# Graph attention feeding a graph convolution: a bias added by an accumulating DMA, and some second-layer tiles computed in rounded halves

## What is computed

```python
# layer 0, per batch                      # layer 1
h  = input @ W                            support = x @ W1 + b
e  = f1 + f2.T          # h@a1, h@a2      y = adj @ support
e  = where(e >= 0, e, 0.2 * e)            mean, var over all batches and nodes
attention = softmax(adj * e, axis=1)      y = relu((y - mean) * rsqrt(var + eps) * gamma + beta)
x  = attention @ h + bias + input         out = y + x
```

## Time and profile before

| | us |
|---|---|
| three runs, median (lowest to highest) | 909.66 (909.13 to 911.93) |
| the profiled execution | 911.96 |
| its span, first to last instruction | 910.2 |
| busy in the span: PE | 871.0 |
| ACT | 804.2 |
| DVE | 726.1 |
| POOL | 211.6 |

### The profile page before, as it was taken

How to read it: one execution, slowest core, us unless ns; L and a number is a source line. 1 busy time by engine, 2 the same in 40 slices (tenths; PEclk the granted TensorE clock), 3 DMA queues, 4 the chain that set the end, 5 groups by cost and what they waited for, 6 DMA issues and landing times.

```text
span 910.2 us, 8919 instructions
## 1 busy us (share of the span) xinstructions
PE 871.0 (96%) x3167; PEld 547.5 (60%) x3167; DVE 726.1 (80%) x794; ACT 804.2 (88%) x614; POOL 211.6 (23%) x166
## 2 busy tenths in 40 slices
PE   6999999999999999999999999999999999999960
PEld 4335556675656756676566756567566765666850
DVE  3655788797878888887877978788888978879966
ACT  5998699988999799998999889997999979997645
POOL 0012214250333112341142401341113411323000
PEclk9999999999999999999999999999999999999995
DMA  8996676748677595867767495775957677565988
GB/s 337 422 362 240 260 291 237 292 165 334 224 273 268 203 360 173 294 234 267 280 237 300 155 357 207 267 274 199 358 174 292 231 263 287 192 224 190 423 335 344
DMA packets 46220, 246.39 MB, mean 271 GB/s; under 512 B 5560, under 2 KB 6184, under 8 KB 19552
## 3 DMA queue, kind: packets, MB, share of 16 engines
q1 hardware_dynamic: 46176, 245.82, 71.7%
HBM read 221.57 MB, written 24.23 MB: 270 GB/s over the span
## 4 chain that ended last, share of the span: by engine, by line
PE 83%; DVE 7%; ACT 3%; issue 2%; DMA 2%; SPq 1%; POOL 0%; DVEq 0%; ACTq 0%; POOLq 0%
PE acc L526 40%; PE acc L499 10%; PE acc L493 10%; PE acc L495 10%; DVE exp_lo L765 4%; PE acc L480 4%; PE acc L507 2%; PE acc L454 2%; PE acc L539 1%; PE acc L542 1%; PE acc L541 1%; ACT scores L623 1%; DMA adj_slot<-biasT 1%; DVE stats L786 1%; ACT hi L637 1%
## 5 line engine op out<-in xcount | busy, mean ns | idle before, releaser
L746 DVE CUSTOM_DVE_ANT_0 scores<-scores,adj_slot 128x2048 f32<-128x2048 f32 x128 | 297.5, 2324 | 77.5 <-ACT scores L616 30.2
L765 DVE SCALAR_TENSOR_TENSOR exp_lo<-scores,rz,hi 128x2048 fp32r<-128x2048 f32 (+1 forms) x133 | 280.5, 2125 | 0.0
L616 ACT ACTIVATE scores<-adj_slot,f_cols 128x2048 f32<-128x2048 f32 x128 | 255.0, 1998 | 15.4 <-PE acc L499 11.8
L623 ACT ACTIVATE scores<-scores,neg_mx 128x2048 f32<-128x2048 f32 x128 | 255.1, 1993 | 14.2 <-DVE neg_mx L749 14.2
L637 ACT ACTIVATE hi<-scores,rz 128x2048 fp32r<-128x2048 f32 (+1 forms) x133 | 227.5, 1726 | 33.6 <-DVE rz L758 30.4
L526 PE MATMUL acc<-adj_slot,region_even 128*128 128x512 f32 x512 | 228.8, 592 | 0.0
L526 PE MATMUL acc<-adj_slot,region_odd 128*128 128x512 f32 x392 | 175.3, 592 | 0.8 <-DVE region_odd L801 0.8
L526 PEld LDWEIGHTS acc<-adj_slot,region_even 128*128 128x128 f32 x512 | 96.7, 190 | 99.7 <-issue 95.7
L499 PE MATMUL acc<-exp_lo,h_hi 128*128 128x512 f32 x448 | 121.5, 391 | 0.8 <-DVE exp_lo L765 0.7
L526 PEld LDWEIGHTS acc<-adj_slot,region_odd 128*128 128x128 f32 x392 | 74.0, 190 | 77.2 <-issue 73.2
L495 PE MATMUL acc<-hi,h_hi 128*128 128x512 f32 x448 | 119.9, 390 | 0.0
(11 more groups left out here) (77 smaller groups left out, 614.7 us busy)
## 6 DMA issues: line engine op xcount, KB each, us to landing
adj_slot<-adjT SPq DMA_DIRECT2D x159, 1024.0 KB, 5.1
adj_slot<-xT SPq DMA_DIRECT2D x20, 1024.0 KB, 7.6
adj_slot<-biasT SPq DMA_DIRECT2D x32, 256.0 KB, 6.5
xp_dram<-adj_slot SPq DMA_DIRECT2D x32, 256.0 KB, 2.6
adj_slot<-xp_dram SPq DMA_DIRECT2D x8, 1024.0 KB, 12.1
adj_slot<-f_rows SPq DMA_DIRECT2D x7, 1024.0 KB, 6.9
adj_slot<-y_dram SPq DMA_DIRECT2D x7, 1024.0 KB, 12.0
outT<-adj_slot SPq DMA_DIRECT2D x6, 1024.0 KB, 4.7
```

The source lines that it names most:

```text
L616: act.activation(scores[t % ER][:, :], slots[f1_slot(bt.par)][:, :], ACT.Prelu, bias=f2_cols[:, bt.n, t:t + 1], alpha=ALPHA).then_inc(edge ...
L623: act.activation(scores[e][:, :], scores[e][:, :], ACT.Exp, bias=neg_mx[:, e:e + 1], accum_out=zsum[:, e:e + 1]).then_inc(exp_done, 1)
L746: dve.tensor_tensor_reduce(scores[e][:, :], scores[e][:, :], slots[s][:, :], 1.0, NEG_BIG, ALU.mult, ALU.max, mx[:, e:e + 1]).then_inc(max ...
L765: dve.scalar_tensor_tensor(exp_lo[e][:, part_cols(t, i)], scores[e][:, part_cols(t, i)], rz[:, e:e + 1], hi[m][:, part_cols(t, i)].bitcast ...
```

## The change

**The bias.** Its four loads and POOL's four adds go. Once the residual has landed, POOL issues one DMA that adds the bias from DRAM to it in SBUF. `make_xp` waits for that DMA for all four chunks.

**Lent slots.** Slot 9, no longer the bias's, and slots 2, 3 and 4 are given to tiles by parity (`SWAP`): tiles 2, 3 and 4 of a batch take the slots that tiles 9, 11 and 10 of the batch before do not need any more in layer 0, and so are loaded before the batch begins (`load_early`). Tiles 8, 9, 10 and 11 of the previous batch are loaded again at k = 3, 4, 5 and 6.

**Halves.** In a steady batch the second-layer tiles k = 3, 7, 9, 11 and 14 (only 11 and 14 where batch 0 is the previous one: 32 tiles in all) are computed in three float32r passes (`layer1_halves`). The rounded half of the tile comes by a DMA of POOL's queue that rounds on the way (`load_hi`), a second 1 MB read of the tile, into a slot lent for it. DVE makes the low half in place (`tile_low`, one 128 x 2048 instruction each), at its steps 1, 4, 6, 8 and 11, and POOL makes the halves of the tile's 128 columns of support (`split_support`, two instructions each). The slots of tiles 2 and 3 lent for halves are loaded again at k = 11 and 9, which are 14 more 1 MB loads on SP's queue over the kernel.

```diff
+    HI_AT = {3: T_F, 7: 2, 9: 3, 11: 2, 14: T_HI}
+    LOW_STEP = {3: 1, 7: 4, 9: 6, 11: 8, 14: 11}
+    RELOAD = {T_F: 3, T_HI: 4, T_X: 5, T_RES: 6}
...
+            def load_early(nx, t):
+
+                wait_lent(nx.prev(), SWAP[t])
+                load_adj(nx, t)
...
-                        if t >= PRE:
+                        if t >= PRE and k > 2:
                             load_adj(bt, t)
-                        elif not is_last(bt):
+                        elif t < PRE and not is_last(bt):
                             load_adj(nx, t)
-                        if k == 1:
-                            load_again(pv, T_F)
-                        if k == 2:
-                            load_again(pv, T_BIAS)
-                        if k == 3:
-                            load_again(pv, T_X)
+                        for t in RELOAD:
+                            if RELOAD[t] == k:
+                                load_again(pv, t)
+                        for t in LENT:
+                            if LENT[t] == k:
+                                load_again(bt, t)
...
+                if not is_last(bt):
+                    load_early(nx, 2)
+                    load_early(nx, 3)
                 store_xp(bt)
+                if not is_last(bt):
+                    load_early(nx, 4)
...
+            def layer1_halves(bt, k):
+
+                t = SIGMA[k]
+                tile_hi = slots_lo[hi_slot(bt, k)]
+                pe.wait_ge(part_lo_done, split_no(bt, k))
+                pe.wait_ge(hi_loaded[k], hi_value(bt, k))
+                for c in range(NC):
+                    pe.matmul(acc1[c][:, :], part_lo[bt.par][:, tile_cols(t)], tile_hi[:, cols(c)], start=False, stop=False)
+                for c in range(NC):
+                    pe.matmul(acc1[c][:, :], part_hi[:, :], tile_hi[:, cols(c)], start=False, stop=False)
+                pe.wait_ge(tile_lo_done, split_no(bt, k))
+                for c in range(NC):
+                    mm = pe.matmul(acc1[c][:, :], part_hi[:, :], slots_lo[l1_slot(bt, t)][:, cols(c)],
+                                   start=False, stop=False)
+                mm.then_inc(l1_tile, 1)
...
+            def tile_low(bt, k):
+
+                t = SIGMA[k]
+                if t in again_loaded and (bt.n > 0 or t not in LENT):
+                    dve.wait_ge(again_loaded[t], again_value(bt, t))
+                else:
+                    dve.wait_ge(slot_loaded[slot_of(bt.par, t)], adj_value(bt, t))
+                dve.wait_ge(hi_loaded[k], hi_value(bt, k))
+                dve.tensor_tensor(slots_lo[l1_slot(bt, t)][:, :], slots[l1_slot(bt, t)][:, :],
+                                  slots_lo[hi_slot(bt, k)][:, :].bitcast(F32), ALU.subtract).then_inc(tile_lo_done, 1)
...
-            def add_bias(bt, c):
+            def load_hi(bt, k):
+
+                nx = bt.next()
+                if HI_AT[k] == T_F:
+                    pool.wait_ge(edge_out, NT * (bt.n + 1))
+                else:
+                    pool.wait_ge(max_done, NT * nx.n + HI_AT[k] + 1)
+                    for u in HI_AT:
+                        if u < k and HI_AT[u] == HI_AT[k]:
+                            wait_l1(pool, bt, u)
+                pool.dma_start(slots_lo[hi_slot(bt, k)][:, :], adjT[bt.n, tile_cols(SIGMA[k]), :])\
+                    .then_inc(hi_loaded[k], 16)
...
+            def add_bias(bt):
                 pool.wait_ge(res_loaded, 16 * (bt.n + 1))
-                pool.wait_ge(bias_loaded[c], 16 * (bt.n + 1))
-                pool.tensor_tensor(res_sb[:, cols(c)], res_sb[:, cols(c)], bias_sb[:, cols(c)], ALU.add)\
-                    .then_inc(xb_done, 1)
+                pool.dma_start(res_of(bt)[:, :], biasT, accum_op=ALU.add).then_inc(xb_done, 16)
```

More of the change, by code:

```diff
@@ L572, in step @@
                     for c in range(NC):
-                        make_h(nx, x1_sb if is_first(bt) else xn_sb, acc1, c)
+                        make_h(nx, x1_sb if is_first(bt) else xp_of(bt), acc1, c)
                 for c in range(NC):
@@ L823, in step @@
                         exp_low(bt, t)
+                    for k in (() if is_first(bt) else halved(bt.n - 1)):
+                        if LOW_STEP[k] == t:
+                            tile_low(bt.prev(), k)
                 if not is_last(bt):
```

138 lines of the change are left out of this document (98 added, 40 removed).

## The result

The changed kernel takes 925.58 us (median; 922.91 to 927.74), the kernel before on the same chip 909.98 (909.13 to 911.93): a ratio of 1.016, 95% interval 1.013 to 1.019. It is slower, by 15 us; the forecast was 901 (889 to 917), faster. The profiled execution took 923.7 us, its span is 921.9.

A forecast was written before the change was run, and what follows sets the result against it. PE was taken as the bound; a batch is 102.4 + 1.6 of waits + 0.6 for POOL = 104.6 us. Six batches save 8.1, the two-tile stretch 1.2, batch 0 costs 1.0: 901 us median, range 889 to 917.

The forecast's parts named there:

- the floors that follow from 0.69 a tile: PE: each halved tile takes 2.74 instead of 3.43 us; five lower a batch's floor from 105.8 to 102.4 us.
- DVE's wait at a batch's start for tile 2: Batch start: 2.89 us before tile 2's product, counted as gone with the early load, worth nothing on PE.
- The walk: One batch priced step by step from its first second-layer matmul: PE loses 1.6 us behind DVE, 104.0 us.
- The first wait: DVE before k = 7's tile_low: idles 2.7 us for a reload landing after 7.0; PE then loses 0.6 us.
- The rival that ended slower: Pairs at k = 3 to 6 land late, use up the gain from about 8.4 us; 919 us in all, 24%.
- The step that failed: From step 9 on: float32 tiles give DVE 6.17 us for 4.9, so PE no longer waits.
- It fits: Added DMAs: 48 MB more, mean share 0.90, 331 GB/s a steady batch against 386 reached in a slice.
- which I priced at nothing: PE waiting on POOL's halves: split_support of k = 9 done by 47 us at 1.5 each, PE at 50.
- Batch 0's end: Where the bias is awaited: residual issued at 85.0, bias landed at 92, second layer at 95.6 to 96; +1.0 us.

The follow-up runs named there:

- e_no_halves: The changed kernel without any halved tile, all second-layer tiles in float32, moved loads and accumulating bias DMA kept; 917.87 us, ratio 1.0070 to the kernel before.
- e_two_tiles: The changed kernel with two halved tiles (k = 11 and 14) in every batch instead of five in six of them; 910.57 us, ratio 0.9984.
- e_two_spread: e_two_tiles with f1, next x and lent tile loaded later, batch 0's f1 and residual ahead of tiles 0 and 1, POOL's new order; 902.17 us.
- e_five_last: e_five_x13 with lent tile 2 brought back at k = 15 instead of 13; 894.78 us, ratio 0.9821 to the kernel before.
- e_pool_order: The changed kernel with POOL's split_support(9) ahead of split_h(4), and split_support(11) and load_hi(14) ahead of split_h(5); 919.45 us, ratio 1.0085.
- e_five_old_pool: e_five_x13 with POOL's instructions back in the changed kernel's order; 917.91 us, ratio 1.0061 to the kernel before.
- e_bias_only: The kernel before with only the bias edit: accumulating DMA instead of four loads and POOL's four adds; 912.90 us, ratio 1.0014.
- e_low_small: The changed kernel with tile_low over 128 of 2048 columns, the third pass reading the rounded half instead of the low one; 907.96 us, ratio 0.9957.
- e_three_spread: e_two_spread with k = 3 halved too, three halved tiles; 907.93 us, ratio 0.9958 to the kernel before.
- e_five_x13: e_five_spread with the next batch's x loaded at k = 13 instead of 14; 903.28 us, ratio 0.9893 to the kernel before.
- e_three_last: e_three_spread with next x at k = 13 instead of 14 and lent tile 2 back at k = 15 instead of 13; 897.84 us, ratio 0.9853.
- the two with a part taken back: e_five_x13 with reloads back at k = 3 to 6 (918.49 us), and e_five_x13 with POOL's old order (917.91 us).
- e_five_spread: e_two_spread with five halved tiles, lent tile 3 back at k = 11, tiles 9, 8, 11, 10 reloaded at k = 1, 3, 4, 5; 903.80 us.

## Why the prediction was wrong

**What held.** The new float32r passes take 0.91 to 0.92 us, and the floors that follow from 0.69 a tile were reached: 104.4 with two tiles. `tile_low` has a median of 2.29 us (2.27 taken), DVE is busy 97 to 98 us in a full batch (98.7 taken), and DVE's wait at a batch's start for tile 2 is gone. The walk was right up to its first wait: DVE is free for k = 7's `tile_low` at 26.9 us (26.8), the reload is issued at 22.3 (22.4).

**The first wait** came much as forecast: 2.7 us before k = 7's `tile_low`, on a reload that lands after 7.0. In the six batches with five halved tiles that reload landed after 6.8, 8.5, 6.9, 6.9, 7.0 and 7.1 us, and DVE stood 2.3, 4.0, 2.4, 2.7, 2.5 and 2.6. The longest is in the batch shown above:

```profile
344.00 2.29 DVE L837 TENSOR_TENSOR adj_lo<-adj_slot,adj_lo 128x2048 fp32r<-128x2048 f32 x1 [4.01 <-DMA adj_slot<-adjT]
```

The rival that ended slower (24%, 919 us) put the lateness into these same pairs, from a landing of 8.4 us on; that held in this one batch. Late loads are its mechanism, but for the most part not at its place.

**The step that failed** is the one after it: "From step 9 on the float32 tiles give DVE 6.17 us for 4.9 and PE no longer waits", resting on "It fits". The mean share was forecast well (0.90; measured 0.87, over a longer batch). But a mean share says nothing of a tile's own landing. The walk has no wait of DVE on a `score`; measured are 17.8 us of them in the five full batches, 3.6 a batch, against the 3.0 by which a batch was longer than forecast (107.6 for 104.6). Tile 12, loaded at k = 10, landed after 7.2 to 9.2 us and cost DVE 0.9 to 3.6 in each; tile 15, loaded at k = 13, after 7.4 to 8.4 and 0.7 to 1.9. Both are issued where a slot comes free and used at once. The walk looked at the pairs at k = 3 to 6 and not at the later places, although the diff shows the lent reloads and the earlier trace rows a slice at 0.98. The kernel before had 3.0 us of such waits a batch too, with 18 us of slack on DVE to hide them. With DVE at 98.7 of a 102.4 us batch the whole slack was 3.7 us, and the first wait used most of it. e_no_halves shows the late loads apart from the engines' work; e_two_tiles against e_two_spread, and the changed kernel against e_five_last, show it together with POOL's order.

**POOL.** "which I priced at nothing": 1.5 us for each instruction, done by 47. The four behind the rounding load took 1.94 to 2.65 and ended at 52.6. The two of them that come first in e_pool_order show the stretch: the cast takes 0.30 us there and 2.35 in the changed kernel, where DVE ran its two-input instructions without a gap. The Trainium skill (SBUF — State Buffer, the section on the shared port) says that the two wait for each other's instruction to end; 2.3 us, one long DVE instruction, agrees. In the changed kernel this was hidden by the loads; in e_five_old_pool it is a part, of unknown size, of 3.3 us a batch. So the price was wrong, and the forecast did not fail by it: with POOL's order alone put right the batches stayed at 107.7.

**Batch 0's end** was +1.0 (-1 to +4) and came at +4.9. The accumulate took 8.37 us (7 taken, 5 to 10), from 85.11 (85.0 taken), so it landed at 93.5 instead of 92: 1.5 of the 3.9 us that were missed. PE, which had stood for 2.78 us by then, took 5.47 us for `make_support`. Its line in PE's timeline, and the window around it (granted clock third from the end), in the changed kernel:

```profile
94.33 5.47 PE L557 MATMUL acc<-w_sb,adj_slot 128*128 128x128 f32 x32 [2.78 <-DVE adj_slot L874]
```

```profile
93.00:100.00 7.00, 5.67 (x33) 5.50 (x34) 4.80 (x9) 3.83 (x2) 0.32 (x1) 0.76 0.40 110
```

The same in e_two_tiles, where PE stood 0.93 us:

```profile
92.33 3.84 PE L557 MATMUL acc<-w_sb,adj_slot 128*128 128x128 f32 x32 [0.93 <-DVE adj_slot L874]
```

```profile
92.00:99.00 7.00, 6.67 (x39) 5.01 (x40) 6.80 (x10) 3.92 (x3) 0.83 (x2) 1.00 0.53 141
```

5.47 - 3.84 = 1.6 us of the miss is the granted clock of 0.76, the mean of a window of which part ran at 1.2 instead of 2.4 GHz. The last 0.8 I take to be that `make_support` follows `make_xp` piece by piece more slowly than its last chunk alone, which I had counted. Which clock a kernel gets there varies with a microsecond of landing: of the kernels with this order of loads the accumulate went out at 84.4 to 85.1 us in those whose `make_support` took 5.46 or 5.47 (the changed kernel, e_bias_only, e_no_halves, e_low_small) and at 82.4 to 83.6 in the others, whose batch 0 ended at 95.6 to 96.5, within 1 us of the forecast. It is also in e_three_spread, e_five_x13, e_three_last and the two with a part taken back. So most of this miss belongs to the execution that was profiled. That is why differences of 2 to 4 us between whole runs don't tell of the batches, and why the table gives the batches apart.

**Open.** Why the reload of the batch shown took 8.5 us to land, 1.4 more than any of the other five, was not found. Of the moves that e_five_spread makes together, f1's and the lent reload's were not tried alone. Why the last full batch keeps its gain (103.8) was not tested; its DMA share of 0.80 suggests the missing loads of a next batch.

## What to carry to other kernels

Whether added traffic fits is decided place by place: list, for each step, what is issued in it from every queue, and when the next load that somebody waits for stands behind it; a mean DMA share of 0.87 and of 0.90 went with 107.6 and 103.5 us. When an engine is filled to its last few per cent, each wait of it for a load is paid in full, so spread the loads before adding the work. And when several waits stand one behind another, taking away one alone can show nothing: remove all, then put each back.

## What the runs showed of the hardware

- A DMA that adds 1 MB from DRAM to SBUF lands after 8.4 to 12.5 us (median 11.6) in the changed kernel, up to 13.7 in e_five_last. A DMA that rounds on the way lands like a plain one: median 6.7 us for 1 MB, beside 7.0 for the reloads. Issuing costs POOL 0.9 and 0.57 us.
- Landing times are not what counts: in e_five_last the reloads' median is 9.0 us and in the changed kernel 7.0, and the former is faster by 31 us, since no engine waits for them. The reloads' landings, changed kernel first, then e_five_last:

```profile
DMA to landing us min/median/max: 4.9/7.0/9.7
```

```profile
DMA to landing us min/median/max: 4.8/9.0/13.1
```
